# First keys and values in pieces, raw keys out of PSUM, and FFN outputs by chunk of rows in a transformer block on one Trainium2 core

## The reference

```python
mod = (silu(c) @ wmod).reshape(4, 6, 1, 1024)      # c: (4, 1024), wmod: (1024, 6144)
sa, ca, ga, sb, cb, gb = mod[:, 0], ..., mod[:, 5]
ga, gb = sign(g) * max(|g|, 0.25) of each
h = layernorm(x) * (1 + ca) + sa                   # x: (4, 1024, 1024), float32
q, k, v = split(h @ Wqkv + bqkv)                   # Wqkv: (1024, 3 * 256)
a = softmax(q @ k.T / 16) @ v
x = x + ga * (a @ Wo + bo)
h = layernorm(x) * (1 + cb) + sb
x = x + gb * (h @ weight.T + bias + lora(h))       # weight: (1024, 1024), one of three rank-16 adapters by batch
```

## Time and profile before

| | us |
|---|---|
| median of 3 runs | 1042.85 (1041.23 to 1042.93) |
| the profiled execution | 1042.57 |
| its span, first to last instruction | 1040.8 |
| TensorE busy | 1011.5 |
| VectorE busy | 663.6 |
| ScalarE busy | 309.2 |
| GpSimd busy | 231.2 |

### The profile page before, as it was taken

How to read it: one execution, slowest core, us unless ns; L and a number is a source line. 1 busy time by engine, 2 the same in 40 slices (tenths; PEclk the granted TensorE clock), 3 DMA queues, 4 the chain that set the end, 5 groups by cost and what they waited for, 6 DMA issues and landing times.

```text
span 1040.8 us, 12891 instructions
## 1 busy us (share of the span) xinstructions
PE 1011.5 (97%) x5158; PEld 831.6 (80%) x5158; DVE 663.6 (64%) x827; ACT 309.2 (30%) x460; POOL 231.2 (22%) x182
## 2 busy tenths in 40 slices
PE   4899999999999999999999999999999999999996
PEld 1677777888888889888898888888887888888885
DVE  4866756498744398532976548776688578566622
ACT  1422333123232132420234523322432333142300
POOL 0000000423201322004230034342223315042411
PEclk9899999999999999999999999999999999999999
DMA  9987574767102553024443146565553646463421
GB/s 348 409 317 244 211 295 140 252 227 265 70 1 77 207 197 127 1 94 157 155 162 117 41 142 225 203 220 184 200 202 126 216 145 202 140 225 122 142 76 66
DMA packets 54475, 180.74 MB, mean 174 GB/s; under 512 B 5784, under 2 KB 6352, under 8 KB 54416
## 3 DMA queue, kind: packets, MB, share of 16 engines
q1 hardware_dynamic: 45152, 146.35, 40.9%
q0 software_dynamic: 9104, 33.04, 8.4%
q10 hardware_dynamic: 160, 0.53, 0.1%
HBM read 146.25 MB, written 33.65 MB: 173 GB/s over the span
## 4 chain that ended last, share of the span: by engine, by line
PE 91%; DMA 4%; DVE 2%; SPq 1%; issue 1%; POOL 0%; ACT 0%; DVEq 0%; POOLq 0%; ACTq 0%
PE pairC L1370 8%; PE pairA L1370 8%; PE pairC L1371 8%; PE pairC L1372 7%; PE pairA L1371 7%; PE pairA L1372 7%; PE pairD L1370 7%; PE pairD L1371 7%; PE pairD L1372 7%; PE pairB L1370 5%; PE pairB L1371 5%; PE pairB L1372 5%; DMA z_cols<-in_x_cols 2%; PE pairB L1526 1%; PE pairD L1478 1%; PE pairA L1478 1%
## 5 line engine op out<-in xcount | busy, mean ns | idle before, releaser
L923 POOL TENSOR_TENSOR xr<-xr,row_bc 128x1024 f32<-128x1024 f32 x32 | 79.9, 2503 | 110.1 <-DMA xr<-in_x 90.3
L936 POOL TENSOR_TENSOR res<-res,row_bc 128x1024 f32<-128x1024 f32 x32 | 81.7, 2565 | 83.4 <-DMA res<-x_dram 76.9
L1370 PE MATMUL pairC<-w_hi,h_hi 128*128 128x512 f32 (+1 forms) x256 | 90.1, 352 | 0.0
L1371 PE MATMUL pairC<-w_lo,h_hi 128*128 128x512 f32 (+1 forms) x256 | 90.0, 351 | 0.0
L1372 PE MATMUL pairC<-w_hi,h_lo 128*128 128x512 f32 (+1 forms) x256 | 89.6, 350 | 0.0
L1370 PE MATMUL pairD<-w_hi,h_hi 128*128 128x512 f32 (+1 forms) x224 | 77.6, 346 | 0.0
L1371 PE MATMUL pairD<-w_lo,h_hi 128*128 128x512 f32 (+1 forms) x224 | 77.6, 346 | 0.0
L1372 PE MATMUL pairD<-w_hi,h_lo 128*128 128x512 f32 (+1 forms) x224 | 77.2, 345 | 0.0
L928 POOL DMA_DIRECT2D x_dram<-xr x32 | 18.0, 562 | 229.3 <-DVE xr L1276 229.3
L1079 ACT ACTIVATE w_hi<-w_sum 128x1024 fp32r<-128x1024 f32 x32 | 33.8, 1059 | 100.5 <-DVE w_sum L1320 100.2
L1370 PE MATMUL pairB<-w_hi,h_hi 128*128 128x512 f32 (+1 forms) x160 | 59.8, 374 | 0.0
...
## 6 DMA issues: line engine op xcount, KB each, us to landing
...
```

What stands on the lines that cost most here:

```text
L923: nc.gpsimd.tensor_tensor(xt, xt, row_bc[:, :], ALU.add).then_inc(residual_made, 1)
L936: nc.gpsimd.tensor_tensor(rt, rt, row, ALU.add).then_inc(residual2_made, 1)
L1370: nc.tensor.matmul(out, left[0], right[0], start=first, stop=False)
L1371: nc.tensor.matmul(out, left[0], right[1], start=False, stop=False)
```

## The change

1. **The first batch's statistics.** `BCP` is split in `BCM` (means, as soon as the four `ST` are there) and `BCP` (roots), 4 matmuls each, and both chunks of batch 0 go this way. ScalarE copies both out of PSUM into SBUF (`BMC`, `BPC`), and `Z` reads the copy. The transpose `RT0(0,1)` and its way through HBM are gone.
2. **The scale in blocks of columns.** Part 0 of the modulation is loaded as eight pieces of 4 x 128 rows by 256 columns (same bytes, rows of 1 KB instead of 4 KB) and made in four blocks: `M0(c)`, `MC0(c)`, `MT0(c)`, `MM0(c)`. `HH(0,0,k)` waits only for block k. `M0` has 8 matmuls of 256 columns in four column groups. Later parts use four buffers in turn; before, the second part used six.
3. **First keys and values by pairs.** The values of the first chunk come in four pieces `V0(c)` of 24 matmuls, beside `K0(c)`. The halves of the weights are loaded and split as k, v, k, v, q, q.
4. **Keys raw out of PSUM.** For batch 0, `KR` (ACT) copies the keys to SBUF without bias, the pair of banks is free then, and `KH` and `KL` read that copy.
5. **FFN by chunk of rows.** `f_no` becomes 8b + 4j + 2h + p: all output columns of a chunk of rows before the next chunk.
6. **All five lists are written anew**; among others `SI` moves from behind the first `ST` and `WQL` to the front of `DVE_ORDER`, the two halves of q's weights to the back of the first loads, and `K0(3)` behind `Q(0,0,1)`.

```diff
-PARTS = ((1, 0), (1, 1), (0, 0), (0, 1), (2, 0), (2, 1))
+PARTS = ((1, 0), (2, 0), (1, 1), (2, 1), (0, 0), (0, 1))
...
 PE_ORDER = [
-    ("BCP", (), "A", None), ("M", (0, 0), "B", None), ("M", (0, 1), "B", None), ("M", (0, 2), "B", None),
-    ("M", (0, 3), "B", None), ("MT", (0,), "B", None), ("K0", (0,), "C", None), ("K0", (1,), "C", None),
...
+    ("BCM", (0,), "A", None), ("BCP", (0,), "A", None), ("M0", (0,), "B", None), ("MT0", (0,), "B", None),
+    ("M0", (1,), "C", None), ("MT0", (1,), "C", None), ("K0", (0,), "D", None), ("M0", (2,), "A", ("BCM", 0)),
+    ("V0", (0,), "B", ("M0", 0)), ("M0", (3,), "C", ("M0", 1)), ("V0", (1,), "B", None), ("MT0", (2,), "A", None),
+    ("MT0", (3,), "C", None), ("K0", (1,), "D", None), ("K0", (2,), "D", None), ("BCP", (1,), "A", ("M0", 2)),
+    ("V0", (2,), "B", None), ("M", (1, 0), "C", ("M0", 3)), ("BCM", (1,), "A", None), ("M", (1, 1), "C", None),
+    ("V0", (3,), "B", None), ("Q", (0, 0, 0), "A", ("BCM", 1)), ("M", (1, 2), "C", None), ("M", (1, 3), "C", None),
+    ("Q", (0, 0, 1), "A", None), ("MT", (1,), "C", None), ("M", (2, 0), "B", ("V", 0, 0)), ("K0", (3,), "D", None),
+    ("M", (2, 1), "B", None), ("SAM", (), "C", ("M", 1)), ("K", (0, 1, 0), "D", ("K", 0, 0)),
+    ("K", (0, 1, 1), "D", None), ("M", (2, 2), "B", None), ("M", (2, 3), "B", None),
+    ("RT0", (1, 0), "D", ("K", 0, 1)), ("SAT", (), "C", None), ("Q", (0, 1, 0), "D", ("RT0", 1, 0)),
+    ("TWM", (), "C", ("SAM",)), ("MT", (2,), "B", None), ("M", (3, 0), "A", ("Q", 0, 0)), ("TWT", (), "C", None),
+    ("M", (3, 1), "A", None), ("RT", (0,), "B", ("M", 2)), ("Q", (0, 1, 1), "D", None), ("M", (3, 2), "A", None),
+    ("V", (0, 1, 0), "B", ("RT", 0)), ("M", (3, 3), "A", None), ("V", (0, 1, 1), "B", None),
...
-    ("WQH", (1, 0), None), ("MC", (0,), "B"), ("WQH", (1, 1), None), ("HH", (0, 0, 0), None), ("WQH", (0, 0), None),
-    ("WQH", (0, 1), None), ("HH", (0, 0, 1), None), ("HH", (0, 0, 2), None), ("HH", (0, 0, 3), None),
...
+    ("WQH", (1, 0), None), ("BMC", (0,), "A"), ("BPC", (0,), "A"), ("MC0", (0,), "B"), ("HH", (0, 0, 0), None),
+    ("MC0", (1,), "C"), ("WQH", (2, 0), None), ("WQH", (1, 1), None), ("HH", (0, 0, 1), None), ("MC0", (2,), "A"),
+    ("WQH", (2, 1), None), ("MC0", (3,), "C"), ("HH", (0, 0, 2), None), ("WQH", (0, 0), None),
+    ("WQH", (0, 1), None), ("HH", (0, 0, 3), None), ("BPC", (1,), "A"), ("BMC", (1,), "A"), ("HH", (0, 1, 0), None),
...
-    ("ST", (0, 0), None), ("ST", (0, 1), None), ("ST", (0, 2), None), ("ST", (0, 3), None), ("WQL", (1, 0), None),
-    ("SI", (), None), ("Z", (0, 0, 0), "A"), ("Z", (0, 0, 1), "A"), ("Z", (0, 0, 2), "A"), ("MM", (0,), "B"),
...
+    ("SI", (), None), ("ST", (0, 0), None), ("ST", (0, 1), None), ("ST", (0, 2), None), ("ST", (0, 3), None),
+    ("WQL", (1, 0), None), ("Z", (0, 0, 0), None), ("MM0", (0,), "B"), ("HL", (0, 0, 0), None),
+    ("Z", (0, 0, 1), None), ("WQL", (2, 0), None), ("MM0", (1,), "C"), ("WQL", (1, 1), None),
+    ("HL", (0, 0, 1), None), ("Z", (0, 0, 2), None), ("ST", (0, 4), None), ("ST", (0, 5), None), ("MM0", (2,), "A"),
+    ("MM0", (3,), "C"), ("ST", (0, 6), None), ("HL", (0, 0, 2), None), ("ST", (0, 7), None), ("WQL", (2, 1), None),
+    ("Z", (0, 0, 3), None), ("WQL", (0, 0), None), ("WQL", (0, 1), None), ("HL", (0, 0, 3), None),
...
-    ("LN", 0, 0), ("LN", 0, 1), ("Lsm",), ("LN", 0, 2), ("LN", 0, 3), ("Lid",), ("LWq", 1, 0), ("LT", 0, 0, 0),
-    ("LT", 0, 0, 1), ("Lwm", 0, 0), ("Lwm", 0, 1), ("Lwm", 0, 2), ("Lwm", 0, 3), ("Lwm", 0, 4), ("Lwm", 0, 5),
-    ("Lwm", 0, 6), ("Lwm", 0, 7), ("LT", 0, 0, 2), ("LWq", 1, 1), ("LT", 0, 0, 3), ("LWq", 0, 0), ("LWq", 0, 1),
...
+    ("LN", 0, 0), ("LN", 0, 1), ("Lsm",), ("LN", 0, 2), ("LN", 0, 3), ("Lid",), ("LT", 0, 0, 0), ("LWq", 1, 0),
+    ("Lwm", 0, 0), ("Lwm", 0, 1), ("LT", 0, 0, 1), ("Lwm", 0, 2), ("Lwm", 0, 3), ("LWq", 2, 0), ("LT", 0, 0, 2),
+    ("Lwm", 0, 4), ("Lwm", 0, 5), ("LWq", 1, 1), ("LT", 0, 0, 3), ("Lwm", 0, 6), ("Lwm", 0, 7), ("LWq", 2, 1),
+    ("LN", 0, 4), ("LN", 0, 5), ("LN", 0, 6), ("LN", 0, 7), ("LT", 0, 1, 0), ("LT", 0, 1, 1), ("LT", 0, 1, 2),
...
-            return n if n < 8 else (n - 8) % 6 if n < 16 else n % 4
+            return n if n < 8 else n % 4
...
-            return 8 * b + 4 * h + 2 * j + p
+            return 8 * b + 4 * j + 2 * h + p
...
+            elif what == "K" and i[0] == 0:
+                eng.wait_ge(k_raw_made, 2 * i[1] + 2)
...
+                    if s == CA:
+
+                        half, at = k % 2, q * H + k // 2 * 2 * P
+                        src = wmod[half * BANK:(half + 1) * BANK, at:at + 2 * P].rearrange("(k p) n -> p k n", p=P)
+                        sp.dma_start(wm[k].rearrange("p (k n) -> p k n", k=4), src).then_inc(ld_wm[k], 16)
...
+                elif what == "MC0":
+                    c = i[0]
+                    act.wait_ge(mod_used, 2 * c + 2)
+                    wait(act, ca_turned, c - 1)
+                    nc.scalar.activation(mod_rows[:, c % 2 * 2 * P:(c % 2 + 1) * 2 * P], ps[:, 0:2 * P], ACT.Copy).then_inc(ca_copied, 1)
+                elif what in ("BMC", "BPC"):
+
+                    j = i[0]
+                    if what == "BMC":
+                        act.wait_ge(mean_spread, j + 1)
+                    else:
+                        act.wait_ge(stat_spread, j + 1)
+                    wait(act, z_made, 4 * j)
+                    cols = slice(0, CHUNK) if what == "BMC" else slice(CHUNK, 2 * CHUNK)
+                    nc.scalar.activation(bc[:, cols], ps[:, cols], ACT.Copy).then_inc(spread_copied, 1)
...
+                elif what == "KR":
+
+                    _, j, m = i
+                    act.wait_ge(k_done, 2 * j + m + 1)
+                    act.wait_ge(mod_used, 6)
+                    nc.scalar.activation(k_raw[:, m, j * CHUNK:(j + 1) * CHUNK], ps[:, m * BANK:(m + 1) * BANK],
+                                         ACT.Copy).then_inc(k_raw_made, 1)
...
+                    raw = what == "KH" and b == 0
...
+                    if raw:
+                        act.wait_ge(k_raw_made, 2 * j + m + 1)
+                    src = k_raw[:, m, j * CHUNK:(j + 1) * CHUNK] if raw else ps[:, m * BANK:(m + 1) * BANK]
...
+                elif what == "MM0":
+                    c = i[0]
+                    dve.wait_ge(ca_turned, c + 1)
+                    nc.vector.tensor_scalar(modT[:, PLACE[CA], :, 2 * c:2 * c + 2],
+                                            ps[:, BANK:BANK + 2 * B].rearrange("p (c b) -> p b c", b=B), 1.0, None,
+                                            ALU.add).then_inc(ca_made, 1)
...
+                    if b == 0:
...
+                        dve.wait_ge(spread_copied, 2 * j + 2)
...
+                elif what == "M0":
+
+                    c = i[0]
+                    if c == 0:
+                        pe.wait_ge(c_ready, 1)
+                    for k in range(CT):
+                        if k % 4 == 0:
+                            pe.wait_ge(ld_wm[2 * c + k // 4], 16)
+                        q = 32 * (k % 4)
+                        last = nc.tensor.matmul(ps[q:q + 32, 0:2 * P], scT[:, k * B:k * B + 32],
+                                                wm[2 * c + k // 4][:, k % 4 * 2 * P:(k % 4 + 1) * 2 * P],
+                                                start=(k < 4), stop=(k >= 4))
+                        if k % 4 == 3:
+                            last.then_inc(mod_used, 1)
...
+                elif what == "MT0":
+                    c = i[0]
+                    pe.wait_ge(ld_const, 16)
+                    pe.wait_ge(ca_copied, c + 1)
+                    for cc in range(2):
+                        at, col = BANK + B * cc, c % 2 * 2 * P + cc * P
+                        last = nc.tensor.matmul(ps[:, at:at + B], mod_rows[:, col:col + P], sel, start=True, stop=True)
+                    last.then_inc(ca_turned, 1)
...
+                elif what in ("BCM", "BCP"):
+
+                    j = i[0]
                     pe.wait_ge(ld_const, 16)
-                    pe.wait_ge(rstd_made, 1)
-                    for k in range(2):
-                        for t in range(4):
-                            at = k * CHUNK + t * P
-                            last = nc.tensor.matmul(ps[:, at:at + P], stat[:, 0, k, t:t + 1].to_broadcast([P, P]), ident,
-                                                    start=True, stop=True)
-                    last.then_inc(stat_spread, 1)
+                    if what == "BCM":
+                        pe.wait_ge(stat_made, 4 * j + 4)
+                    else:
...
+                elif what == "V0":
+
+                    c = i[0]
+                    pe.wait_ge(w_lo_made, PARTS.index((2, c // 2)) + 1)
+                    pe.wait_ge(h0_lo_made, 2 * c + 2)
+                    for ct in range(2 * c, 2 * c + 2):
+                        for t in range(4):
+                            last = product3(ps[:, t * D:(t + 1) * D], both(h_hi[0], h_lo[0], ct, slice(t * P, (t + 1) * P)),
```

(3 more changed lines are left out.)

136 lines of the change are left out of this document (69 added, 67 removed), and 675 rows, old and new, of tables (ACT_ORDER, DVE_ORDER, PE_ORDER, POOL_ORDER).

## The result

The changed kernel is slower: 1048.18 us median of 5 runs (1046.03 to 1052.45) against 1042.17 (1040.75 to 1042.93), a ratio of 1.0070 with a 95% interval from 1.0056 to 1.0083. The forecast was 1041.3 us with a range up to 1046.0. The execution that was profiled is the changed kernel's shortest, 1046.03 us with a span of 1044.2, so its profile shows 3.4 us of the loss and hides the rest; the runs of the changed kernel are spread over 6.4 us, those of before over 2.2. That spread had to be explained too.

What follows compares the result with a forecast made beforehand. TensorE was busy for 97% of the span, its head bound by bytes first, then by the chain from statistics to HL. -0.6 - 1.8 - 0.7 + 1.6 = -1.5 us on 1042.57 gave 1041.1, as median 1041.3; range 1037.0 to 1046.0.

Steps and rivals of the forecast that it cites:

- part 1: Start of the first chain: first real product K0(0) starts at 24.9 us, 5.7 us earlier than at 30.6.
- part 3: Data supply in the head: 1 KB rows take 1.5 us a transfer; the head gives 0.6 us, of 0.1 to 1.0.
- rival D: 1 KB rows in the head are slow: at 2.0 us a transfer M(1,1) waits, 4 us more, 1045.3; chance 0.11.
- (a): Block of small products at 77 to 83.5 us is split, its wait and fallen clock go: -1.8 us, at worst 0.
- (b): Late waits of 0.6 and 0.4 us: FFN by chunk of rows relaxes them, -0.7 us, at worst a new wait of 2.
- (c): New TensorE waits around 42 to 51 us, with one restart at the low clock: +1.6 us.
- rival C: Head products in eight pieces restart at 1.2 GHz; three that count give 5.6 us more, 1046.9; chance 0.14.
- (d): KR frees pair C sooner; LN and M(1) weight loads have four slots, not six, but land before M(1,2): nothing.
- (e): The tail behind the last matmul is the same instructions: nothing.

Runs made afterwards that it cites:

- e4: The changed kernel with V0(2) ahead of BCP(1) on TensorE: 1046.21 us, ratio 1.0045.
- e9: The changed kernel with the edits of e4, e5 and e6 together: 1044.61 us, ratio 1.0029.
- e12: The changed head with the FFN of before, e4, e5, HH and HL(0,0,3) ahead of WQH and WQL, V0(3) and K0(3) ahead of M(1,0): 1043.63 us, 1.0013.
- e16: e12 with six slots for modulation weight tiles 8 to 15, where it had four: 1043.29 us, ratio 1.0017.
- e5: The changed kernel with MM(2) ahead of ST(1,6) in VectorE's queue: 1045.96 us, ratio 1.0043.
- e2: The kernel before with only the FFN part of the change (output numbering and later lists): 1043.68 us, ratio 1.0017.
- e13: The changed kernel with its FFN and all the moves of e12 and e6: 1044.29 us, ratio 1.0017.
- e3: The changed kernel with only its head, output numbering and later lists as in the kernel before: 1045.39 us, ratio 1.0041.
- e8: The changed kernel with matmuls that nobody reads, five ahead of MT0(1) and eight ahead of BCP(1): 1045.96 us, ratio 1.0048.
- e1: The changed kernel measured again with no edit, against the kernel before: 1048.44 us, ratio 1.0060.
- e10: e9 with five matmuls that nobody reads ahead of MT0(1): 1044.41 us, ratio 1.0030.
- e11: The kernel before with eight matmuls that nobody reads ahead of K0(0): 1042.13 us, ratio 1.0006.
- e14: The kernel before with four slots in turn for the modulation weights from the ninth tile on, where it had six: 1049.00 us, ratio 1.0073.
- e15: The changed kernel with six slots for modulation weight tiles 8 to 15, where it had four: 1047.20 us, ratio 1.0046.
- e6: The changed kernel with POOL's addition R2(3,0,1,0) made to wait for VectorE's normalisation NM(14): 1046.70 us, ratio 1.0046.

## Why the prediction was wrong

- **The start (part 1): right.** `K0(0)` was to start at 24.9 us and started at 24.08 to 25.09 in the profiles of this head.
- **1 KB rows (part 3): right, and rival D wrong.** The two stretches of the changed kernel's first profile that hold almost nothing but such rows, against the earlier trace rows:

```profile
22.00:24.00 2.00, 0.35 (x4) 0.39 (x4) 1.34 (x3) 2.00 (x4) 0.00 (x0) 1.00 1.08 351
28.00:30.00 2.00, 2.00 (x22) 1.03 (x21) 1.82 (x3) 1.64 (x4) 0.00 (x0) 0.94 1.10 353
```

  351 to 353 GB/s against 410 is 1.28 x 410 / 352 = 1.49 us for such a load, where I took 1.5, and such loads landed 1.50 us behind the one before (12.92, 14.43, 15.92 us). The last of the eight landed at 31.4 us, forecast 31.5. The other estimate there, 1.37 us, is too low.
- **The head's sum (part 3), -0.6 us: the step that failed first.** Two of its times were late. The first are the landings behind 33 us: `LN(0,4)` was to land at 34.1 us and landed at 35.4, and from there on every load is 1.3 us late, the last of `M(1,1)`'s at 52.0 and not at 50.7. `V0(3)` is queued behind `M(1,1)` and ended at 56.0 us, not at 54.2 to 55.1:

```profile
35.41 1.29 DVE L1224 BATCH_NORM_STATS2 bn<-xr 128x6 f32<-128x512 f32 x2 [2.29 <-DMA xr<-in_x]
...
51.85 1.25 PE L1463 MATMUL pairC<-wm,pads 128*32 128x512 f32 x8
53.04 0.39 PE L1418 MATMUL pairB<-w_hi,h_hi 128*128 128x256 f32 x1
```

  No load lands between 32.6 and 35.4 us, where one is due every 1.28; what held them there is open. The second is the root for `BCP(1)`: I priced it with 1.6 us, as at the start of the kernel before, and it took 3.1, from the last statistics at 42.6 us to 45.7. So `BCP(1)` started at 45.84 us, just behind my range (43.1 to 45.5). POOL and VectorE in the changed kernel, then the same root in the kernel before, where VectorE was idle beside it:

```profile
42.52 1.17 DVE L1213 TENSOR_TENSOR w_lo<-w_raw,w_hi 128x1024 fp32r<-128x1024 f32 x1
42.69 1.07 POOL L931 TENSOR_TENSOR var<-stat,eps 128x4 f32<-128x4 f32 x1 [26.03 <-DVE stat L1227]
43.61 1.22 DVE L1239 TENSOR_TENSOR z_cols<-z_cols,xs 128x1024 f32<-128x1024 f32 x1
43.83 1.87 POOL L933 TENSOR_TENSOR stat<-var,power 128x4 f32<-128x4 f32 x1
```

```profile
47.73 0.20 POOL L909 TENSOR_TENSOR var<-stat,eps 128x4 f32<-128x4 f32 x1 [34.15 <-DVE stat L1179]
48.01 1.01 POOL L911 TENSOR_TENSOR stat<-var,power 128x4 f32<-128x4 f32 x1
```

  All 14 profiles with the changed head have these long roots here and once more at 207 us, and behind those TensorE waits 0.3 to 1.6 us at 210; the kernel before takes 1.3 us for the pair at 48 and at 210 us and waits at neither. No run changed the roots alone, so what they cost is read and not tested; e4 shows that the wait for the first of them was covered by the late loads. With 880 left the first profile is 0.7 us behind, 1.3 us worse than forecast, and this without the half clock behind that wait. The larger mistake is of kind: I set 5.7 us of earlier start against 4.5 us of added work. e4, e9, e12 and e16 show that the lead is worth nothing by itself: a transfer, a step of VectorE or POOL's roots take it each time, at 52 us, then up to 134 us, then at 77 us, and at 210.
- **(a), -1.8 us: right about the clock, refilled at once.** The clock stayed at 1.00 from 80 to 90 us, and a wait of 1.2 us came at 104 us (e5). Between 880 and 800 left the changed kernel makes up only 0.4 us, and by 720 left it has lost 0.5 again, 0.4 of it in a wait at 210 us for POOL's roots that the kernel before does not have. I had not looked behind which transfer the moved `MM(2)` would stand.
- **(b), -0.7 us, at worst +2: wrong sign.** It is +1.8 alone (e2), +0.7 in the mended head (e13 less e12), and +2.5 in the first profile, outside my worst; but e3, with the FFN of before, loses 1.7 there too, so that +2.5 is not all of the edit's making. I had counted instructions of VectorE per tile, and not who stands beside whom: the `WS` of batch 0 (1.4 us of waits against 0.4) and `NM(14)` beside POOL (1.3 us). The table of waits could not have told the second; the durations of VectorE beside POOL's could.
- **(c), +1.6 us: right** in five of seven executions, with 1.3 us measured; the first profile is one of the two without. e8 fits the cause, about 2 us less by the medians for matmuls that nobody reads, though its interval does not tell it from e1. My rival C put more of them in the head and needed two and a half that count. As a mechanism it has part of the loss; e10 and e11 show why its price was wrong, since the first piece's half clock is covered.
- **(d), the slots, nothing: right in this kernel, and by the order of its lists.** The same line costs the kernel before 7.6 us (e14), since `M(1,2)` comes there before its loads. In the changed kernel they land ahead of `M(1,2)`, with four slots as with six (e15), as I had it; e15's median is 1.1 us lower, which its interval does not tell from nothing. In the mended head the slots count: six put it 2.3 us earlier with 720 left (e16 against e12), but the times, 1.0017 and 1.0013, are the same. I had looked at one piece, `M(1,2)` at 60 us, and not at the queue behind the loads that wait, which issues nothing from 41.3 to 50.9 us; that this did no harm here is in part luck.
- **(e), the tail: right.** The last product starts 10.7 us before the end of the span in both.

The first profile has no half clock behind 30 us, so (c) is left out and the forecast for it is 1042.57 - 3.1 = 1039.5 us. Against that, 1.3 us (head) + 1.4 + 0.5 ((a) and what came behind it) + 3.2 ((b), +2.5 for -0.7) are 6.4, which gives 1045.9, and 1046.03 was measured. The sum closes because its terms are differences of the same two timelines; this says where the time went, and not why. With the half clock it is 1047.1 (e1). Where the 1 us from there to the median of 1048.2 lies is open: e5's profile shows one longer execution that lost it in the head, but the runs of the FFN part alone are spread too (e2). What decides between them is open as well. Why three single gains of about 2 us make 3.8 together is answered in part: the wait at 944 us is in e4's gain and in e6's. For the rest the intervals, some 3 us wide, leave room for chance.
